# Three layer-0 feed-forward tiles run on tokens 0 to 511 and then on two parts of 256, and four x loads are issued later

## The reference

```python
x = L0_attn_x
xn = _layernorm(x, axis=-1)                       # mean and variance over the 1024 features
s = _L0_attn_ref(xn, Wz, bz, Wh, bh)              # gate, candidate, scan over tokens
g = _silu(_L0_ffn_ref(xn, w_gate, w_up, w_down))  # int32 weights, scaled by 1/127
x = x + s * g
# inside _L0_ffn_ref:
gate = jnp.einsum('bsd,hd->bsh', x, wg)           # 1024 -> 3072
up = jnp.einsum('bsd,hd->bsh', x, wu)
h = jax.nn.silu(gate) * up
return jnp.einsum('bsh,dh->bsd', h, wd)
```

## Time and profile before

| | us |
|---|---|
| median of 3 runs | 1167.37 |
| lowest, highest | 1166.59, 1343.29 |
| the profiled execution, its time | 1166.48 |
| its span (core 5, the slowest) | 1165.3 |
| spans of the eight cores | 1163.4 to 1165.3 |

### The profile page before, as it was taken

How to read it: one execution, slowest core, us unless ns; L and a number is a source line. 1 busy time by engine, 2 the same in 40 slices (tenths; PEclk the granted TensorE clock), 3 DMA queues, 4 the chain that set the end, 5 groups by cost and what they waited for, 6 DMA issues and landing times.

```text
span 1165.3 us, 15111 instructions; the slowest of 8 cores (1163.4 to 1165.3 us)
## 1 busy us (share of the span) xinstructions
PE 1147.6 (98%) x5382; PEld 524.7 (45%) x5382; DVE 514.4 (44%) x606; ACT 291.1 (25%) x365; POOL 172.5 (15%) x321
## 2 busy tenths in 40 slices
PE   5999999999999999999999999999999999999998
PEld 3444444444444444444444444444444444444444
DVE  4233331555656764225566885011134343343343
ACT  4211111122123111112212723533112133322310
POOL 3222221111111111111011122221000000011121
PEclk8999999999999999999999999999999999999999
DMA  9996688544554675545552678984010112455676
GB/s 215 211 148 97 92 126 182 109 109 101 114 112 73 130 160 77 84 85 99 111 108 52 93 125 156 153 154 117 1 19 19 37 37 46 87 117 118 139 177 168
DMA packets 91401, 126.90 MB, mean 109 GB/s; under 512 B 48192, under 2 KB 48448, under 8 KB 91328
## 3 DMA queue, kind: packets, MB, share of 16 engines
q0 software_dynamic: 35200, 77.61, 40.6%
q1 hardware_dynamic: 56128, 48.33, 15.7%
HBM read 159.47 MB, written 20.97 MB: 155 GB/s over the span
## 4 chain that ended last, share of the span: by engine, by line
PE 98%; DMA 2%; DVE 0%; ACT 0%; issue 0%; SPq 0%; DVEq 0%; ACTq 0%; POOLq 0%
PE PS L156 97%; DMA S<-wg 1%; DMA S<-xtok 1%; PE PS L293 0%; ACT S L281 0%; DVE S L160 0%; ACT S L309 0%; DVE S L284 0%; SPq L127 0%; DVE S L889 0%; DVEq L63 0%; ACTq L63 0%; POOLq L63 0%
## 5 line engine op out<-in xcount | busy, mean ns | idle before, releaser
L156 PE MATMUL PS<-S 128*128 128x512 bf16 x5264 | 1135.9, 379 | 1.3 <-DMA S<-wg 1.3
L156 PEld LDWEIGHTS PS<-S 128*128 128x128 bf16 x5264 | 515.0, 98 | 620.2 <-issue 5.4
L160 DVE TENSOR_TENSOR S<-S,PS 128x512 bf16<-128x512 bf16 x96 | 66.0, 688 | 179.6 <-PE PS L156 170.2
L404 ACT ACTIVATE S<-PS 128x512 bf16<-128x512 f32 x96 | 57.3, 597 | 259.0 <-PE PS L156 192.9
L855 ACT ACTIVATE S<-PS,CB 128x2048 bf16<-128x2048 f32 x16 | 31.5, 1968 | 182.4 <-DVE CB L850 182.4
L848 DVE TENSOR_REDUCE CB<-PS 128x1 f32<-128x1024 f32 x32 | 39.2, 1225 | 72.3 <-PE PS L156 72.3
L127 POOL DMA_DIRECT2D S<-x1s x32 | 17.3, 539 | 337.2 <-DVE S L889 313.1
L127 POOL DMA_DIRECT2D S<-wg x48 | 28.7, 598 | 232.6 <-PE PS L156 230.0
L480 ACT ACTIVATE S<-PS 128x512 bf16<-128x512 f32 x32 | 19.1, 597 | 172.9 <-PE PS L156 172.9
L748 DVE SCALAR_TENSOR_TENSOR S<-S,PS 128x1024 f32<-128x1024 f32 x16 | 19.5, 1221 | 80.8 <-PE PS L156 79.7
L160 DVE TENSOR_TENSOR S<-PS,S 128x512 f32<-128x512 f32 (+1 forms) x33 | 22.3, 676 | 66.9 <-PE PS L156 66.6
(11 more groups left out here) (72 smaller groups left out, 429.9 us busy)
## 6 DMA issues: line engine op xcount, KB each, us to landing
S<-wg POOLq DMA_DIRECT2D x48, 256.0 KB, 5.1
S<-wu POOLq DMA_DIRECT2D x48, 256.0 KB, 5.8
S<-wd POOLq DMA_DIRECT2D x16, 768.0 KB, 8.0
S<-xtok SPq DMA_DIRECT2D x16, 512.0 KB, 9.9
S<-xt SPq DMA_DIRECT2D x16, 512.0 KB, 16.1
x1s<-S SPq DMA_DIRECT2D x16, 512.0 KB, 2.6
S<-x1s POOLq DMA_DIRECT2D x32, 256.0 KB, 5.9
out<-S SPq DMA_DIRECT2D x31, 256.0 KB, 4.8
```

The source lines that it names most:

```text
L156: ins = te.matmul(dst, l, r, start=(i == 0), stop=(i == n - 1))
L160: return DVE.did(ve.tensor_mul(o, a, b))
L404: at = ACT.did(se.activation(sil, ps(bg), AF.Silu, scale=1.0 / 127.0))
```

## The change

It does four things. Loads of x tiles 4 to 7 leave their place behind tile 3: SP now waits for weight load 1, issues 4 and 5, waits for weight load 3, issues 6 and 7, and only then the small constants `cb` and `ones`. The statistics of tiles 4 and 5, the normalisation of 4 and the weight loads 6 and 7 go from ahead of the first matmul to behind the first `gate_up`. The first hidden tiles done on span 0 alone are three, not four; the same three then run on tokens 512 to 767 and then on tokens 768 to 1023, in matmuls of 128x256, so that tile 3 of the hidden features does both spans in the normal order. And the transposes of tiles 4 to 7 move: 4 and 5 between gate and up of the third call, 6 in the middle of the fifth, 7 behind it.

```diff
         xk_load(0)
         i_tok = dma(SYN, ident[:], identd, i_sem)
-        for i in range(1, 8):
+        for i in range(1, 4):
             xk_load(i)
-        c_tok = dma(SYN, CB[:, 0:32], cb, c_sem)
-        c_tok = dma(SYN, ones[:], onesd, c_sem)
...
         w_pair()
         w_pair()
+
+        for i, k in ((4, 1), (6, 3)):
+            SYN.after(w_tok[k])
+            xk_load(i)
+            xk_load(i + 1)
+        c_tok = dma(SYN, CB[:, 0:32], cb, c_sem)
+        c_tok = dma(SYN, ones[:], onesd, c_sem)
...
-        ln0_stats(4)
-        ln0_rstd(4)
-        ln0_bias(4)
-        ln0_norm(4, True)
-        ln0_stats(5)
-        ln0_rstd(5)
-        ln0_bias(5)
-        w_pair()
-
-
-        def span1_a():
-            ln0_norm(5, True)
+
+
+        def early_a():
+            ln0_stats(4)
+            ln0_rstd(4)
+            ln0_bias(4)
+            ln0_norm(4, True)
+            ln0_stats(5)
+            ln0_rstd(5)
+            ln0_bias(5)
+            w_pair()
+
+        def early_b():
+            ln0_transpose(4)
+            ln0_transpose(5, True)
+
+        def early_c():
             ln0_stats(6)
             ln0_rstd(6)
             ln0_bias(6)
-
-        def span1_b():
-            ln0_transpose(5)
             ln0_norm(6, True)
             ln0_stats(7)
             ln0_rstd(7)
 
-        early0 = [span1_a, span1_b, lambda: ln0_norm(7), lambda: None]
-        early0_mid = [None, lambda: ln0_transpose(4), lambda: ln0_transpose(6), lambda: ln0_transpose(7, True)]
+
+        early0 = [early_a, lambda: ln0_norm(5, True), early_c, lambda: ln0_norm(7), lambda: ln0_transpose(7, True)]
+        early0_mid = {2: early_b, 4: lambda: ln0_transpose(6)}
...
-        def gate_up(h, m, s, k, mid=None):
+        def gate_up(h, m, s, k, mid=None, part=None):
+            lo, hi = (0, 512) if part is None else (part * 256, part * 256 + 256)
...
-            order = [(m, s) for m in range(NM) for s in range(2)]
+            order = [(m, s, None) for m in range(NM) for s in range(2)]
             if h == 0:
-                order = [(m, 0) for m in range(4)] + [(m, 1) for m in range(4)] + order[8:]
-            for n, (m, s) in enumerate(order):
+                order = [(m, s, p) for s, p in ((0, None), (1, 0), (1, 1)) for m in range(3)] + order[6:]
+            for n, (m, s, part) in enumerate(order):
...
-                first = h == 0 and n < 8
-                mm = gate_up(h, m, s, k, early0_mid[n] if first and n < 4 else None)
-                if first and n < 4:
+                first = h == 0 and n < 9
+                mm = gate_up(h, m, s, k, early0_mid.get(n) if first else None, part)
+                if first and n < 5:
                     early0[n]()
-                if first and n == 3:
+                if first and n == 4:
                     SYN.after(w_tok[7])
...
-                if s == 1:
+                if s == 1 and part != 0:
                     w_done(k, mm)
                     w_done(k + 1, mm)
```

More of the change, by code:

```diff
@@ L394, in xn_span @@
             return S[:, XN + h * 8192 + c * 1024 + s * 512:XN + h * 8192 + c * 1024 + (s + 1) * 512]
-        def gate_up(h, m, s, k, mid=None):
+        def gate_up(h, m, s, k, mid=None, part=None):
+            lo, hi = (0, 512) if part is None else (part * 256, part * 256 + 256)
             PE.after(w_tok[k])
             bg = bank()
-            mm = mms(ps(bg), [(w_tile(k, c), xn_span(h, c, s)) for c in range(NC8)])
+            g = ps(bg)[:, 0:hi - lo]
+            mm = mms(g, [(w_tile(k, c), xn_span(h, c, s)[:, lo:hi]) for c in range(NC8)])
             q = hs_slot[0]
             hs_slot.rotate(-1)
-            sil = bf(HS + q * 512, 512)
+            sil = bf(HS + q * 512, hi - lo)
             ACT.after(mm, hs_free.popleft())
-            at = ACT.did(se.activation(sil, ps(bg), AF.Silu, scale=1.0 / 127.0))
+            at = ACT.did(se.activation(sil, g, AF.Silu, scale=1.0 / 127.0))
             bank_free[bg] = at
@@ L409, in gate_up @@
             bu = bank()
-            mm = mms(ps(bu), [(w_tile(k + 1, c), xn_span(h, c, s)) for c in range(NC8)])
+            u = ps(bu)[:, 0:hi - lo]
+            mm = mms(u, [(w_tile(k + 1, c), xn_span(h, c, s)[:, lo:hi]) for c in range(NC8)])
             DVE.after(mm, at)
-            vt = mul(bf(HB + m * 1024 + s * 512, 512), sil, ps(bu))
+            vt = mul(bf(HB + m * 1024 + s * 512 + lo, hi - lo), sil, u)
             bank_free[bu] = vt
@@ L625, in build_program @@
         for h in range(2):
-            order = [(m, s) for m in range(NM) for s in range(2)]
+            order = [(m, s, None) for m in range(NM) for s in range(2)]
             if h == 0:
-                order = [(m, 0) for m in range(4)] + [(m, 1) for m in range(4)] + order[8:]
-            for n, (m, s) in enumerate(order):
+                order = [(m, s, p) for s, p in ((0, None), (1, 0), (1, 1)) for m in range(3)] + order[6:]
+            for n, (m, s, part) in enumerate(order):
                 k = wpos + 2 * m
                 if m == 0:
-                    for i in range(8 * h + 4 * s, 8 * h + 4 * s + 4):
+                    t0, nt = 8 * h + 4 * s, 4
+                    if part is not None:
+                        t0, nt = t0 + 2 * part, 2
+                    for i in range(t0, t0 + nt):
                         PE.after(xn_tok[i])
-                first = h == 0 and n < 8
-                mm = gate_up(h, m, s, k, early0_mid[n] if first and n < 4 else None)
-                if first and n < 4:
+                first = h == 0 and n < 9
+                mm = gate_up(h, m, s, k, early0_mid.get(n) if first else None, part)
+                if first and n < 5:
                     early0[n]()
-                if first and n == 3:
+                if first and n == 4:
                     SYN.after(w_tok[7])
@@ L642, in build_program @@
                         xk_load(i)
-                if first and n == 7:
+                if first and n == 8:
                     DVE.after(c_tok)
```

## The result

The changed kernel is slower, by about twice what was forecast. Its four runs gave 1174.33, 1175.14, 1199.67 and 1254.14 us; in the last two, as in some runs of most kernels here, the cores of a die ran at a lower granted clock, and every time and ratio from here on leaves such runs out. The ratio to the kernel before is 1.0069, interval 1.0040 to 1.0098, or +8 us. The profiled execution took 1174.33 us. `x4` is x tile 4.

What follows compares the result with a forecast made beforehand. TensorE was taken as the bound, waiting only in the opening. Terms -1.8 - 1.2 + 2.3 + 3.3 + 0.6 + 0.1 + 1.2 = +4.5 us on the profiled 1166.48 gave 1171.0 us; range 1167.0 to 1174.0.

Steps and rivals of the forecast that it cites:

- The wait before tile 6: Before tile 6's transposes: PE waits 3.3 us, its statistics standing behind the third product on DVE; the largest term.
- Before tile 7: Before tile 7's transposes: PE waits 0.6 us more, as its normalisation comes after a held product on DVE.
- The 256-column parts: 96 matmuls of 256 columns for 48 of 512: +0.1 us taken, between nothing and +0.4.
- Tile 6's gate weights: Second round of weights: PE wants hidden tile 6's gate at 68.8 us, it lands near 71.0; a 2.2 us wait.
- the clock, set to 0: Opening, core 5's half-rate stretch: 0 us taken, bounded by it being gone (-1.7) or a second one following (+1.8).
- the clock falls again: Rival, chance 0.15: the new, longer PE waits bring half rate again, 1.8 us on top, 1172.8 us.
- where x tiles 4 and 5 land does not matter: Wait before tiles 4 and 5: x tiles issued near 17 us, DVE not wanting them before 24; no cost.
- 2.3 was said: Before the transposes of tiles 4 and 5: PE waits 2.3 us, their statistics standing behind the first product on DVE.
- the start, -1.8: PE's first real matmul: 1.1 us earlier by a faster first weight load, 0.7 by tile 1 landing earlier.
- the -0.7: Part of the start: tile 1 lands earlier with fewer loads behind it; bounds 0 and -1.9 us.
- Second round, +1.2: Weight loads after the opening: later weight load 7 and x tiles 8 to 15 make PE wait; 1.2 us taken.
- The 1172.8 by that rule: Forecast total in us if TensorE, left idle between bursts, returns to half rate, by the Trainium skill's page.

Runs made afterwards that it cites:

- experiment 4: Changed kernel with the statistics of tiles 6 and 7 moved behind the second call, normalisation of 6 still behind the third; 1175.62 us, ratio 1.0078.
- 15: Kernel before with only the 256-column parts and new transpose places, `wd` loads behind the fourth hidden tile; 1165.60 us, ratio 0.9994.
- experiments 1: Changed kernel with x tiles 4 to 7 loaded at the start again, everything else kept; 1173.74 us, ratio 1.0059.
- experiment 5: Changed kernel with the two `wd` loads issued behind the fourth hidden tile again instead of the third; 1174.53 us, ratio 1.0067.
- experiments 3: Changed kernel with 8, 24 and 48 unread matmuls ahead of the transposes of tiles 4, 5 and 6; 1176.26 us, ratio 1.0084.
- experiment 13: Changed kernel with the `wd` loads behind the fourth hidden tile and 8, 24 and 48 unread matmuls in its three waits; 1172.94 us, ratio 1.0055.
- experiment 9: Changed kernel with x tiles 4 and 5 issued behind weight load 0 instead of 1; one run, 1174.15 us.

## Why the prediction was right in direction and wrong in size

**Right, and shown.** That behind the opening nothing changes per matmul (1119.1 us again). The wait before tile 6: 3.3 said, 3.41 measured, 3.43 to 3.45 on most cores of every kernel with this order of DVE and nothing filled in, gone in experiment 4 and absent in 15. Before tile 7, 0.6 said; 0.52 and 0.51 on cores 1 and 2 where the half rate doesn't hide it. The 256-column parts: 0.1 said, nothing found. No wait for a weight at the start. Tile 6's gate weights as the next bound after the opening: said for 69 us, found at 73 to 74 on three cores, 1.4 us at most.

**The step that failed first: the clock, set to 0.** It was +3.7 us on the slowest core. I took one stretch at the lower level as a thing that comes and goes, and bounded it by one more. The rival "the clock falls again" had a chance of 0.15 and the price of one stretch; the slowest core got two more, worth 1.7 us each, and its first covered 0.6 us more of matmuls than before. The rows for it were there: an idle of 1.85 us and half rate behind it. In this kernel every core pauses three times within 15 us, and every core fell.

**The second: "where x tiles 4 and 5 land does not matter".** I had them issued near 17 us and landed before 24, at a pace like that of the earlier trace rows. They were issued at 15.6 to 19.1, and x5 landed at 28.8 on core 7 (27.6 in the median) and DVE waited for it. What stood between are weight loads that POOL had issued before: x4's first packet came 2.1 to 4.3 us behind its issue. DVE's order alone costs 0.53 + 1.42 = 1.95 us before tiles 4 and 5 (experiments 1 and 5); the late tiles add 0.4 on core 7 and 0.7 to 2.0 on the others, whose waits are 2.65 to 3.90 us. That core 7 has 2.36 where 2.3 was said is luck. Its first matmuls ran at half rate, so the product ahead of the statistics came 2.0 us later, as did the end of the 40 matmuls, and x5 was only 0.78 us too late for DVE.

**The third: the start, -1.8.** It was -0.5 on the slowest core against the slowest of before, and nothing between the medians of eight cores (19.75 against 19.73). The wait for weight load 0 did go, but PE is then released by the copy of tile 2, which no load shortens (that was said), and tile 1 landed no earlier: at 7.9 to 9.7 us on the eight cores, median 9.1, and before at 7.5 to 9.3, median 8.1. Core 5, from which the -0.7 was taken, was the latest of the eight.

**Second round, +1.2.** 0 on the slowest core, up to 1.4 on others, and its real weight was another: in experiments 3 and 4 it takes back what is won in the opening. x8 was issued at 36.2 to 39.5, where 36 was said.

**Together** on the slowest core: the start 1.3 us worse than the term, the clock 3.7, the ends of merged rows 0.2, tiles 4 to 6 0.2, tile 7 -0.6, the small matmuls -0.1, the second round -1.2. That is +3.5 to the 4.5 of the sum, and the spans differ by 8.0. The range ended at 1174.0 because I let only one of the rivals come at a time, although the half rate came behind waits, and a fuller queue makes waits.

The sum follows one core, and the time is that of the slowest. Core 0 has one stretch at 0.50 of 3.4 us and yet a span of 1172.8, only 0.5 us less than core 7: it starts at 20.68, waits 3.42 us before tiles 4 and 5, 3.44 before tile 6 and 1.36 for weights at 74 us. So the clock is the largest missing term on core 7, but taking it away alone would not have saved 3.7 us, and in experiment 3 it saved nothing.

The Trainium skill's page "TensorE: Matmul & The Clock Gate", section "HAM oscillation — how this bites in real kernels", says that a TensorE left idle between bursts of matmuls goes back to half rate and pays the warming again. The traces of the changed kernel agree on all eight cores, on core 7 even behind gaps of 0.53 and 1.83 us with only the eight transposes of tile 4, 0.61 us, between them. But core 1 of experiment 5 had 0.53, 1.42 and 3.44 us and kept its clock. The 1172.8 by that rule was nearer than the sum.

## What to carry to other kernels

Where several engines' queues meet in one opening, price the bounds that stand behind each other before pricing an edit: here no single repair gained beyond its interval, a pair halved the loss, and leaving the placement as it was gave all of it back. Count late cores, not mean ones: when eight cores wait for data, the slowest decides, and each new idle of TensorE like those here, of 1.4 to 3.8 us, should be given the price of a half-rate stretch as a real chance. A load that is issued later is also queued behind what was issued meanwhile, and an instruction that waits for it holds everything that is written behind it on its engine, even for another tile.

## What the runs showed of the hardware

- A pause decides little about the clock by its length alone. After 3.43 to 3.45 us before tile 6 the first experiment had a stretch at 0.50 close behind it on cores 0, 1, 4 and 6, and none on cores 2, 5 and 7. Core 1 of experiment 5 had none at all. The stretches in these traces lasted some 3.4 or 6.8 us.
- Unread matmuls held the clock in most places: with 8, 24 and 48 of them no core of experiment 3 fell between 24 and 75 us, against all eight without. With the same ones in experiment 13, three cores fell near 31 us, behind 2.2 to 2.3 us of idle that was left beside them.
- An x load issued by SP moved no byte for 2.1 to 4.3 us (eight cores of the changed kernel; 3.9 on core 6 of experiment 9) while POOL's earlier weight loads filled the engines. On that core 6 it then took turns with them, 208 packets to 209 in 5 us. The Trainium skill's page "DMA: Bandwidth & Descriptors", section "Queues, rings and completion order", says that a DMA engine takes turns between its queues packet by packet. The 208 to 209 agree with that; the time before doesn't, and no run here shows why.
